# The dense middle stage of a gated two-layer attention kernel, run tile by tile inside the second attention's loop

## The reference, cut to what matters

```
x = x + tanh(g_xattn[0]) * L0_attention(LN(x), ctx)   # linear attention: kv = k'^T v, per head; dense, LN
x = x + tanh(g_ffn[0])   * L0_ffn(LN(x))              # BitLinear: rows and weights quantised, silu(gate)*up, down
x = x + tanh(g_xattn[1]) * L1_attention(LN(x), ctx)   # softmax attention, 16 heads of depth 8, 1500 keys
x = x + tanh(g_ffn[1])   * L1_ffn(LN(x))              # 8 experts, top 2
```

## Time and profile before

| | us |
|---|---|
| median of 3 runs | 823.58 (821.81 to 823.68) |
| the profiled execution's own time | 823.98 |
| its span, first to last instruction | 822.2 |
| TensorE busy | 701.6 (85%) |
| VectorE busy | 553.2 (67%) |
| ScalarE busy | 494.2 (60%) |
| GpSimd busy | 232.3 (28%) |
| mean granted TensorE clock | 0.929 of 2.4 GHz |

### The profile page before, as it was taken

One profiled execution on the slowest core, in us unless ns is written; L12 is line 12 of the kernel. 1 busy time (PEld: TensorE's weight loads), 2 busy tenths in 40 slices (PEclk: granted clock), 3 DMA queues, 4 the chain that ended last, 5 costly groups with the idle time before them and its releaser, 6 DMA issues.

```text
span 822.2 us, 19580 instructions
## 1 busy us (share of the span) xinstructions
PE 701.6 (85%) x7276; PEld 485.1 (59%) x7277; DVE 553.2 (67%) x1100; ACT 494.2 (60%) x721; POOL 232.3 (28%) x234
## 2 busy tenths in 40 slices
PE   3699999874454689999999999999999999699997
PEld 2577777661313156566655666566655666467786
DVE  5799999965878758676777767777687775421111
ACT  4577777751243447667777677766777677344431
POOL 3488888870100412112220222202221110000000
PEclk9899999985657579999999999999999999699999
DMA  3123222526600262477445764467445561111110
GB/s 131 37 84 105 75 75 75 161 74 31 126 0 1 64 142 53 109 160 157 93 100 127 158 124 101 95 154 158 102 100 114 120 138 37 46 26 42 52 38 23
DMA packets 59459, 74.16 MB, mean 90 GB/s; under 512 B 35308, under 2 KB 40166, under 8 KB 59422
## 3 DMA queue, kind: packets, MB, share of 16 engines
q1 hardware_dynamic: 59422, 73.65, 38.3%
HBM read 32.61 MB, written 1.40 MB: 41 GB/s over the span
## 4 chain that ended last, share of the span: by engine, by line
PE 58%; DVE 23%; issue 10%; ACT 4%; SPq 1%; DMA 1%; POOL 1%; DVEq 1%; ACTq 0%
DVE mx L1236 8%; PE ps L608 7%; PE ps L499 7%; PE ps L678 6%; PE ps L666 6%; PE ps L491 6%; PE ps L595 6%; PE ps L485 6%; PE ps L434 3%; DVE ss L1038 3%; PE ps L448 2%; PE ps L520 2%; ACT arena L743 2%; DVE arena L1058 2%; PE ps L400 1%
## 5 line engine op out<-in xcount | busy, mean ns | idle before, releaser
L1236 DVE TENSOR_REDUCE mx<-ps 128x1 f32<-128x500 f32 x336 | 214.4, 674 | 88.9 <-PE ps L499 87.7
L840 ACT ACTIVATE P<-ps,kbias,kscale 125x896 f32<-125x896 f32 x192 | 210.5, 1098 | 72.0 <-PE ps L595 67.7
L499 PE MATMUL ps<-KP,Qb 128*128 128x500 bf16 x336 | 132.2, 394 | 9.8 <-issue 4.4
L933 POOL TENSOR_TENSOR KP<-kvall,KP 128x1500 bf16<-128x1500 f32 x16 | 48.5, 3033 | 317.9 <-ACT KP L793 317.9
L608 PE MATMUL ps<-P,Vp 125*32 125x112 f32 x3072 | 113.4, 265 | 1.8 <-ACT P L840 1.3
L434 PE MATMUL ps<-wkv,cT 128*125 128x256 f32 x384 | 91.7, 382 | 1.0 <-ACT arena L756 1.0
L608 PEld LDWEIGHTS ps<-P,Vp 125*32 125x32 f32 x3072 | 67.1, 109 | 39.3 <-issue 31.5
L434 PEld LDWEIGHTS ps<-wkv,cT 128*125 128x125 f32 x384 | 69.2, 190 | 10.0 <-issue 1.4
L595 PEld LDWEIGHTS ps<-QS,KS 128*128 128x128 bf16 x768 | 54.1, 99 | 34.8 <-issue 19.0
L595 PE MATMUL ps<-QS,KS 128*128 128x112 bf16 x768 | 68.7, 215 | 5.6 <-DVE QS L1242 5.1
L788 ACT ACTIVATE KP<-ps,bk_sb 128x500 bf16<-128x500 f32 x48 | 32.5, 677 | 66.2 <-PE ps L485 66.2
(11 more groups left out here) (192 smaller groups left out, 981.1 us busy)
## 6 DMA issues: line engine op xcount, KB each, us to landing
cT<-ctxT_dram SPq DMA_DIRECT2D x32, 750.0 KB, 4.5
KS<-KP SPq DMA_DIRECT2D x48, 375.0 KB, 7.3
arena<-KP SPq DMA_DIRECT2D x48, 375.0 KB, 7.2
QS<-QD SPq DMA_DIRECT2D x96, 28.0 KB, 5.7
wgu<-w_dram SPq DMA_DIRECT2D x8, 256.0 KB, 2.8
silu<-w_dram SPq DMA_DIRECT2D x8, 256.0 KB, 2.8
x<-xh_dram SPq DMA_DIRECT2D x1, 512.0 KB, 3.2
mixed<-att SPq DMA_DIRECT2D x16, 28.0 KB
```

Of the source, the lines that this page charges most:

```text
L499: ins = nc.tensor.matmul(ps[:, bank, 0:KCW], q[:, 128 * c:128 * c + 128], KP[par][0][:, KCW * k:KCW * k + KCW], start=True, stop=True)
L840: nc.scalar.activation(P[t % 2][0:TK, :].rearrange("p (k n) -> p k n", k=2), src, ACT.Exp, scale=kscale[0:TK, bass.ds(n, 1)], bias=kbias[0 ...
L1236: ins = v.tensor_reduce(mx[:, c, k:k + 1], ps[:, bank, 0:KCW], AX.X, ALU.max)
```

## The change

The middle stage is made for tiles 0 and 1 alone before stage 3. For tiles 2 to 7 it is cut into nine units, AT (transpose of `att`), DE (dense product), XT (transpose of the quantised row), G and U (gate and up), HT (four transposes), DN (down, four matmuls), LT (transpose of the normed row) and Q1 (query projection), which stand in the table of a pair of windows: pair i carries tile i+2, for i from 0 to 5. AT, G, HT, LT and Q1 are "side" units in bank 6; DE, XT, U and DN are "aux" units and take their turn in banks 4 and 5. The 21 MX units are moved: a window has now one MX less in step 1 and MX4 behind DEN, and MX19 and MX20 stand in step 10 (step 9 held the last one).

```
+    [["MX0", "MX1", "V0"], ["MX2", "MX3", "AT"], ["DEN", "MX4", "V1"], ["MX5", "DE", "V2"],
+     ["MX6", "WO", "K0"], ["MX7", "MX8", "MX9"], ["MX10", "MX11", "K1"], ["MX12", "MX13", "MX14"],
+     ["MX15", "XT", "K2"], ["MX16", "MX17", "MX18"], ["MX19", "MX20", "G"], ["SH", None, None]],
+    [["MX0", "MX1", "V0"], ["MX2", "U", "MX3"], ["DEN", "MX4", "V1"], ["MX5", "MX6", "V2"],
+     ["MX7", "WO", "K0"], ["MX8", "MX9", "HT"], ["MX10", "MX11", "K1"], ["MX12", "DN", "MX13"],
+     ["MX14", "MX15", "K2"], ["MX16", "MX17", "MX18"], ["MX19", "MX20", "LT"], ["SH", None, "Q1"]],
...
+CHAIN = ["AT", "DE", "XT", "G", "U", "HT", "DN", "LT", "Q1"]
+ON_SIDE = ["AT", "G", "HT", "LT", "Q1"]
```

```
+            def first_sum(n):
...
+                dve.wait_ge(sem("c_var"), turn(n, 0, 3))
+                v.scalar_tensor_tensor(lin[:, z, :], lin[:, z, :], mv[:, z, 0:1], gmask[:], ALU.subtract,
+                                       ALU.mult).then_inc(sem("lin_ready"), 1)
...
+                dve.wait_ge(sem("rstd_ready"), turn(n, 0, 3))
+                v.scalar_tensor_tensor(x_of(n), lin[:, z, :], rstd[:, z:z + 1], x_of(n), ALU.mult,
+                                       ALU.add).then_inc(sem("x1_ready"), 1)
+                dve.wait_ge(sem("x1_ready"), n + 1)
+                pause()
+                statistics(n, 1, x_of(n))
```

`pause` is a memset of one column. The reciprocal roots are made by GpSimd, one add and one pow on a column of 128 (`deviation`), in place of ScalarE's Sqrt; Silu becomes a Tanh on ScalarE with the rest of the formula in VectorE's `gate`:

```
+                nc.gpsimd.tensor_tensor(sd[:, z:z + 1], mv[:, z, 1:2], (eps_ln if j else eps_in)[:], ALU.add).then_inc(sem("eps_added"), 1)
+                pool.wait_ge(sem("eps_added"), turn(n, j, 3))
+                nc.gpsimd.tensor_tensor(rstd[:, z:z + 1], sd[:, z:z + 1], mhalf[:], ALU.pow).then_inc(sem("rstd_ready"), 1)
...
+                    nc.scalar.activation(silu[:, z, :], ps[:, bank, :], ACT.Tanh,
+                                         scale=cg[:, z:z + 1]).then_inc(sem("tanh_ready"), 1)
```

A K unit is now read once, by ScalarE, which writes the float32 keys into `krest`, frees the bank, waits for that, and copies them to the first part; VectorE subtracts in SBUF, a third at a time:

```
-                v.scalar_tensor_tensor(krest[:, cols], ps[:, bank_of(w, unit), 0:KCW], bk_sb[:], KP[par][0][:, cols],
-                                       ALU.add, ALU.subtract).then_inc(sem("side_free"), 1)
+                nc.scalar.activation(krest[:, cols], ps[:, bank_of(at, unit), 0:KCW],
+                                     ACT.Identity, bias=bk_sb[:]).then_inc(sem("side_free"), 1)
+                act.wait_ge(sem("side_free"), emptied(at, unit))
+                nc.scalar.copy(KP[par][0][:, cols], krest[:, cols]).then_inc(sem("kp1_ready"), 1)
...
+                v.tensor_tensor(krest[:, cols], krest[:, cols], KP[par][0][:, cols],
+                                ALU.subtract).then_inc(sem("rest_ready"), 1)
```

More of the change, by code:

```diff
@@ L56 @@
 MXS = [f"MX{n}" for n in range(CH * KC)]
-PLACES = [["MX0", "MX1", "V0"], ["MX2", "MX3", "MX4"], ["DEN", None, "V1"], ["MX5", "MX6", "V2"],
-          ["MX7", "WO", "K0"], ["MX8", "MX9", "MX10"], ["MX11", "MX12", "K1"], ["MX13", "MX14", "MX15"],
-          ["MX16", "MX17", "K2"], ["MX18", "MX19", "MX20"], [None, None, None], ["SH", None, None]]
-ALL = [u for places in PLACES for u in places if u]
+PLACES = [
[6 rows of a table added]
+]
+ALL = [[u for places in half for u in places if u] for half in PLACES]
 ENDS = ["DEN", "WO"]
-EARLY = ["K0", "K1", "K2", "V0", "V1", "V2", "K0'", "K1'", "K2'"]
+CHAIN = ["AT", "DE", "XT", "G", "U", "HT", "DN", "LT", "Q1"]
@@ L99, in bank_of @@
-def bank_of(w, unit):
-    return 6 if kind(unit) == "side" else 4 + count_at(w, unit)[1] % 2
-def free_of(w, unit):
-    return "side_free" if kind(unit) == "side" else f"aux_free{bank_of(w, unit)}"
-def emptied(w, unit):
-    m, c = count_at(w, unit)
+    n = units(at, k).index(unit)
+    if par and not (fixed(i) and i < 0):
+        n += len(units((i, 0), k))
+    if fixed(i):
+        return 0, n + (before(i, k) if i >= 0 else 0)
+    each = sum(len(units((i, q), k)) for q in range(2))
+    return each, n + before(LOOPED[0], k) - LOOPED[0] * each
@@ L479, in fill @@
+            def fill(at, unit, b, par):
+                bank = bank_of(at, unit)
+                used = emptied(at, unit) - 1
+                if not fixed(used) or used > 0:
+                    pe.wait_ge(sem(free_of(at, unit)), used)
                 if unit[0] == "K":
@@ L585, in scores, with both @@
-            def scores(b, par, t, k, first):
+            def both(*of):
+                for u in of:
+                    for n in range(2):
+                        fill(BEFORE, f"{u}.{n}", n, 0)
+            both("AT", "DE")
+            for unit in ("V0", "V1", "V2"):
+                fill(BEFORE, unit, 0, 0)
+            both("XT", "G", "U")
+            fill(BEFORE, "K0'", 1, 1)
+            both("HT", "DN")
+            fill(BEFORE, "K1'", 1, 1)
+            both("LT")
+            fill(BEFORE, "K2'", 1, 1)
@@ L587, in scores @@
+            both("Q1")
+            def scores(at, t, k, first):
+                b, par = 2 * at[0] + at[1], at[1]
                 n = b * T + t
@@ L1220, in _ @@
[L1220 to L1231 removed]
+            v.tensor_scalar(bmask[:], row[:, B_O, :], th[:, 1:2], None, ALU.mult).then_inc(sem("bo_ready"), 1)
@@ new lines, in _ @@
+            for n in range(2):
+                dense(BEFORE, n)
+            for n in range(2):
+                first_sum(n)
+            for n in range(2):
+                quantise(n)
+            for n in range(2):
+                quantised(n)
+            for n in range(2):
+                gate(BEFORE, n)
+            for n in range(2):
+                hidden(BEFORE, n)
+                hidden_steps(BEFORE, n)
+            for n in range(2):
+                hidden_quantised(n)
+            key_rest(1, 1, 0)
@@ L1232, in empty @@
+            for n in range(2):
+                second_sum(BEFORE, n)
+            for n in range(2):
+                normed(n)
+            key_rest(1, 1, 1)
+            for n in range(2):
+                query_parts(BEFORE, n)
+            key_rest(1, 1, 2)
+            def empty(at, unit, b, par):
+                bank = bank_of(at, unit)
+                dve.wait_ge(sem("aux_ready"), filled(at, unit))
                 if unit[:2] == "MX":
                     c, k = divmod(int(unit[2:]), KC)
-                    if c == 0 and k == 0 and not (isinstance(b, int) and b == 0):
+                    if c == 0 and k == 0 and not (fixed(b) and b == 0):
```

774 lines of the change are left out of this document (477 added, 297 removed).

## The result

The changed kernel takes 820.1 us (median of 18 runs, 816.67 to 822.79) beside 824.34 us for the kernel before (18 runs on the same chips): ratio 0.9944, 95% interval 0.993 to 0.9958. It is faster by 0.6%, where the prediction had 834 us and slower. The profiled execution took 817.71 us, its span 815.8 us, at a mean granted clock of 0.945.

The account below looks back on a forecast made before the run. The prediction took the middle stage as bound by latency and the softmax loop by TensorE. 824.0 - 34.4 (middle stage) + 43 (six pairs) + 1 (windows without a chain) = 834 us, range 808 to 848.

Parts of the forecast that it names:

- the walk: Step-by-step timing of the two-tile middle stage, query product to first MX: 58.9 us in place of 93.3, 34.4 less.
- pow: GpSimd's pow of one column in the roots: taken as 0.3 us, bounds 0.2 to 3.0; a root 0.7 us.
- rival 3: In the loop, Tanh and Exp reload tables, or GpSimd's pow costs over 1 us: slower, 849 us, chance 0.10.
- I walked both windows: Loop waits added for each window of a pair: first +4.1 us, second +3.1, a pair 7.2, six pairs 43.
- places (MX6, ends, less what goes): Loop terms per pair: MX6 wait +0.7, window ends +1.0 and +1.2, waits that go -0.5 in each window.
- TensorE's units, DE's wait for MX4's bank, starts and waits of VectorE's stubs: Loop terms per pair: TensorE's nine added units 0.85 us a window, and DE's wait for MX4's bank 0.7.
- waits for VectorE's chain functions: Loop terms per pair: V0 +0.4, MX11 +1.2, MX13 and XT +0.5, U and DEN +0.2, MX15 +0.65.
- Rival 2: The loop's added waits overlap, half of the stalls remain, a pair costs 4.5 us: faster, 816 us, chance 0.13.
- rival 4: The change is neutral, a pair of loop windows costs 5.5 us more: 823 us, chance 0.04.
- The break-even: Added loop cost per pair of windows from which the change loses: 5.7 us.
- The range: Whole kernel: 808 to 848 us; the forecast's own narrower range was 825 to 845.
- the sign: Whole kernel: slower, 834 us from 824.0; chances slower 0.69, faster 0.27, same 0.04.

Follow-up runs that it names:

- e1: The kernel before with only the MX units moved to the places of the change's second window, no chain units, old key path: 860.2 us, ratio 1.0448.
- e6: The changed kernel with VectorE's third key rest moved behind the maximum in both windows and ScalarE's second key part a step later: 813.8 us, ratio 0.9858.
- e3: The changed kernel without the chain units, functions and roots of tiles 2 to 7, new places and key rests in thirds kept: 796.9 us, ratio 0.9709.
- e14: The changed kernel with each VectorE operation for tiles 2 to 7 replaced by a one-column memset with the same waits and signals: 810.4 us, ratio 0.9832.
- e10: The changed kernel with each of the nine chain units of tiles 2 to 7 issued twice in a row on TensorE: 823.1 us, ratio 0.9986.
- e7: The changed kernel reordered ahead of the loop: dense before key rests, first roots before the third key part, V copies before the second: 817.4 us, ratio 0.9904.
- e5: The changed kernel with VectorE's quantise moved from behind MX8 to behind MX9, and quantised from MX10 to MX11: 818.8 us, ratio 0.9922.
- e4: The changed kernel with MX4 issued and emptied ahead of DEN in both windows of a pair: 816.7 us, ratio 0.9889.
- e15: e12 with query_parts moved ahead of MX0's reduction, hidden_steps behind MX5 and hidden_quantised behind MX7: 801.7 us, ratio 0.9721.
- e11: The changed kernel with the edits of e4, e6 and e7 together: 805.7 us, ratio 0.9775.
- e12: e11 with VectorE's quantise and quantised of the first window cut in halves, placed behind MX7, MX8, MX10 and MX11: 804.1 us, ratio 0.975.
- e9: The changed kernel with VectorE's row operations for tiles 2 to 7 narrowed to one column, all instructions and waits kept: 814.6 us, ratio 0.9888.

## Why the prediction was wrong, point by point

**The middle stage.** The step that failed is the first of the walk: "TensorE then makes K0 to K2 at the low clock: 2.03 us each". At 2.03 us each they would have needed 2.8 us more: they took 1.1 us each in eleven of the thirteen profiles with the new stage, also where the query product took 3.85 us (1.9, 1.1 and 1.7 in the other two). I carried a duration over from a place where the trace shows what had gone before it: TensorE idle for 5.26 us, and then

```profile
191.74 0.58 PE L533 MATMUL ps<-wabs,onesf 128*128 128x3 f32 x2 [5.26 <-DVE wabs L1119]
...
192.74 2.01 PE L485 MATMUL ps<-cT,wk_sb 128*128 128x500 f32 x2
```

(the timeline of TensorE before the change). e1 keeps that stage, and its query product took 2.18 us, at a granted clock of 1.00; behind the idle time its first key product still took 2.01. Now the three stand directly behind 32 products. The granted clock in the stretch of the key products is 0.50 before and 1.00 in e6 (windows view, last but two):

```profile
192.74:202.00 9.26, 6.08 (x7) 1.47 (x7) 2.44 (x6) 1.36 (x3) 0.00 (x0) 0.50 1.14 39
```

```profile
186.45:191.37 4.92, 3.32 (x10) 1.23 (x8) 4.70 (x17) 2.57 (x4) 0.00 (x0) 1.00 0.47 31
```

Held against e6, from the start of the query product:

| step | forecast | e6 |
|---|---|---|
| product for the mask over | 13.2 | 9.3 |
| key rests over | 22.6 | 18.1 |
| first root made | 27.8 | 23.5 |
| first MX | 58.9 | 53.1 |

3.9 of the 5.8 us stand in the first row: 2.8 from the clock (3 times 0.92), and about 1.0 for ScalarE's last read of bank 6, which I put on the path though nothing waits for it. Of the rest, VectorE's block up to the key rests was 0.6 us too long and the steps behind the first root 1.5; the third key part and the root took 0.2 more than forecast. With 2.03 us replaced by 1.1 and the read left out, the walk would have given 55.2. The profiled run's 51.4 us has another 1.7 from its query product: 2.18 us at a granted clock of 1.00, 3.85 in e6 at 0.55.

**pow.** I took 0.3 us with the add inside 0.7 for a root; pow is 0.55 to 0.67 in the kernel after and the add 0.19. A root costs 0.8: right in size. No `ACT_TABLE_LOAD` stands between 180.6 and 690 us; the last one ahead of the Tanh and Exp is at 179.35:

```profile
179.35 1.28 ACT L886 ACT_TABLE_LOAD   x1
```

So rival 3 is out. By the rule of the Trainium skill ("ScalarE: Activation LUTs", "Table sets: the hidden batching unit"), that tanh and exp share a set, there would be none, and the trace agrees.

**The loop.** Here the step that failed is the adding up of the waits for VectorE in "I walked both windows". Forecast 7.2 us a pair, measured 5.61. The runs split it:

| part | forecast a pair | measured a pair | from |
|---|---|---|---|
| places (MX6, ends, less what goes) | 1.9 | 1.94 | e3 against before |
| TensorE's units, DE's wait for MX4's bank, starts and waits of VectorE's stubs | 2.4 | 2.30 | e14 against e3 |
| waits for VectorE's chain functions | 2.95 | 1.37 | after against e14 |

The forecasts are the prediction's own terms: 0.7 + 1.0 + 1.2 - 1.0; twice 0.85, and 0.7; 0.4 + 1.2 + 0.5 + 0.2 + 0.65. The measured parts are differences in one order of removal; in another the shares may shift, as e1 beside e3 shows. By this split the term that was mis-sized is the third, by 1.6 us, the whole of the error of a pair. The split is not clean: the stubs of the second row still hold MX11 for 0.50 us, so that VectorE's part is more than 1.37 us and TensorE's less than 2.30. TensorE's own time says the same of the waits: its idle time rose by 3.0 us a pair (2.3 to 5.3), where the waits of the walk and the ends came to 5.5, and its busy time by 2.6 (50.2 to 52.8), where I had 1.7. I priced each of VectorE's blocks as a wait of nearly its own length and added them. In the trace the waits are there but smaller: V0 0.21 for 0.4, MX11 0.99 for 1.2, XT 0.24 for 0.5, MX15 0.31 for 0.65. And they don't add: an early wait holds TensorE back, VectorE catches up meanwhile, and a later wait is shorter. e10 shows it from the other side, where TensorE's extra work shortened four waits. Rival 2 said that in words, with 4.5 us a pair, and went too far. Outside of the steady pairs, the first pair cost only 4.4 us, and the windows without a chain 2.2, where I had 1.

**Which rival came true.** None whole: the pair came out at 5.6 us, rival 4's size, with a middle stage 5 to 8 us shorter than in the sum of any of my cases, at or just beyond the 40 us that I had given as its bound. The break-even that I gave, 5.7 us a pair, was for a gain of 35 us; with the 40.2 us of a normal run (93.3 to 53.1) it is 6.6, and 5.6 is a win. The range held the time; the sign and the size were wrong.

**Right.** The place of nearly every wait; the 2.1 us from the maximum to the next window (2.22); the first window without a chain near 26.7 (26.91; the second took 27.41); no load of tables; the clock of the loop at 1.00 in the profile of the kernel after; GpSimd's key part ahead of the roots, which e7 took away for 2.6 us.

**Open.** Why the query product found a granted clock of 1.00 and took 2.18 us in three of the thirteen profiles with the new stage, and took 3.8 to 4.1 in the others. Three profiles have one window that is 1.5 us longer than its kind (e5 and e14 in the second-last full one, e4 in another): its granted clock is 0.94 for 1.00, as in e1, with 0.50 in its first 3 us, so these 1.5 us are the clock's; why it falls there is open. The runs of the kernel after, from 816.67 us (mean granted clock 0.950) to 822.79 (0.935), spread with the clock in the same way, but only one of them has a trace here. And whether the places in the first window could be bettered further: no other table was tried.

## What to carry to other kernels

A matmul's duration holds only with the clock of its place: when work moves from behind an idle stretch to behind dense work, look up the granted clock in both places before carrying the number. Where two engines hand two banks back and forth, don't add the waits that you find; order decides. Emptying the added work (e14) tells what the new places and units cost in that order, but gives no floor: e15, with all the work, has a pair of 55.33 us, e14 56.70. Small moves, found by asking where the engine idles and what stands just ahead of the operation that ends the iteration, took away 17 of the 34.5 us that the loop had lost (e15's loop takes 407.1 us). When two windows with the same work differ, look at the granted clock of each before naming a cause. And test such moves together: a move that shows nothing alone can be held up by the very wait that another removes.

## What the runs showed of the hardware

A pow of one column on GpSimd took 0.55 to 0.67 us (0.87 or 0.88 once in each run with e7's order: e7, e11, e12, e15), an add 0.19. On VectorE half or more of a short operation didn't go with its columns: in e9 operations took 0.14 to 0.27 us over one column, the same ones in the kernel after 0.23 to 0.35 over 128. Work that only shifts in time can cost on another engine: where GpSimd's masked query came to lie on an operation of VectorE with both inputs in SBUF, that ended 0.24 us behind it, after 0.88 us in place of 0.39 in e6's window. And a window of the loop that began at a granted clock of 0.50 took 1.5 us more than its like.
